# A second slot table: twelve of the 36 expert pairs moved in among the last chunks of a fused RWKV and mixture-of-experts kernel

## What is computed

```python
def attn(x):                       # an RWKV block on layernorm(x)
    xn = ln(x); xp = shift(xn)
    k, v, r = (mixes of xn and xp) @ Wk, Wv, Wr     # r through a sigmoid
    wkv = scan over the tokens of exp(k)*v and exp(k), one over the other
    x = x + r * wkv @ Wo
    yn = ln(x); kk = relu((0.5*yn + 0.5*shift(yn)) @ Wfk)**2
    return x + sigmoid(yn @ Wfr) * (kk @ Wfv)

def ffn(x):                        # experts, E = 8, H = 256, top 2
    top, idx = top_k(x @ gate_w.T, 2); p = softmax(top)
    h1, h2 = x @ w12[e]            # 2 x 256 columns
    out_e = (silu(h1) * h2) @ w3[e]
    return sum over the two chosen e of p_e * out_e

x = x + attn(layernorm(x)); return x + ffn(layernorm(x))
```

## Time and profile before

| what | value |
|---|---|
| median of 3 runs | 348.77 us (347.84 to 348.89) |
| the profiled execution's own time | 348.16 us |
| its span (first to last instruction) | 346.4 us |
| PE / PE weight load busy | 78% / 61% |
| DVE / ACT / POOL busy | 71% / 56% / 64% |
| granted TensorE clock, mean | 0.899 of full speed |

### The profile page before, as it was taken

One profiled execution on the slowest core, in us unless ns is written; L12 is line 12 of the kernel. 1 busy time (PEld: TensorE's weight loads), 2 busy tenths in 40 slices (PEclk: granted clock), 3 DMA queues, 4 the chain that ended last, 5 costly groups with the idle time before them and its releaser, 6 DMA issues.

```text
span 346.4 us, 6531 instructions
## 1 busy us (share of the span) xinstructions
PE 270.9 (78%) x1697; PEld 211.3 (61%) x1698; DVE 246.0 (71%) x742; ACT 195.6 (56%) x397; POOL 221.2 (64%) x251
## 2 busy tenths in 40 slices
PE   0388699999779699695949635599999999999700
PEld 0134366766547366373735422499999999999700
DVE  3089998989699796997724757066666666666794
ACT  2546578888828667185544322276666666767200
POOL 5233557557857688677788677426666666666680
PEclk9999899999969899697876965899999999999965
DMA  7920000000011110011001113323333333233785
GB/s 263 437 68 0 1 2 31 0 32 32 34 38 38 47 33 31 31 40 54 32 31 62 62 42 108 98 67 91 93 91 88 91 91 86 84 99 89 260 275 211
DMA packets 22411, 29.12 MB, mean 84 GB/s; under 512 B 4318, under 2 KB 15584, under 8 KB 22129
## 3 DMA queue, kind: packets, MB, share of 16 engines
q1 hardware_dynamic: 14832, 13.45, 13.0%
q0 software_dynamic: 4352, 8.47, 7.4%
q10 hardware_dynamic: 3200, 6.90, 5.3%
HBM read 15.09 MB, written 12.14 MB: 79 GB/s over the span
## 4 chain that ended last, share of the span: by engine, by line
issue 33%; POOL 32%; PE 12%; DMA 10%; DVE 7%; SPq 2%; ACT 1%; POOLq 1%; DVEq 0%; ACTq 0%
POOL res_d L429 11%; POOL rows_d L404 10%; DMA x_all<-x 5%; PE p_f L707 2%; POOL x L374 2%; PE p_up L695 2%; POOL rs L350 2%; DMA o_all<-res_d 2%; POOL ysum L381 2%; POOL x_all L358 2%; POOL gated L366 1%; PE p_up L778 1%; POOL rs L390 1%; PE p_up L656 1%; DMA res_d<-yo,result_row 1%
## 5 line engine op out<-in xcount | busy, mean ns | idle before, releaser
L429 POOL DMA_INDIRECT res_d<-yo,result_row x72 | 70.9, 985 | 40.9 <-issue 30.2
L404 POOL DMA_INDIRECT rows_d<-rows,pos x64 | 67.5, 1055 | 21.8 <-issue 21.2
L778 PE MATMUL p_up<-xgT,w_up 128*128 128x128 f32 x576 | 71.7, 279 | 0.0
L778 PEld LDWEIGHTS p_up<-xgT,w_up 128*128 128x128 f32 x576 | 68.6, 196 | 0.0
L1028 DVE SCALAR_TENSOR_TENSOR gate_h<-th,p_up 128x512 f32<-128x512 f32 x36 | 24.8, 688 | 41.3 <-ACT th L586 41.3
L601 ACT ACTIVATE w_up<-w_exp 128x512 f32 x72 | 41.3, 622 | 12.3 <-issue 11.4
L695 PE MATMUL p_up<-ysum,w_sb 128*128 128x512 f32 x64 | 38.5, 713 | 5.6 <-POOL ysum L381 5.6
L586 ACT ACTIVATE th<-p_up 128x512 f32<-128x512 f32 x36 | 21.5, 597 | 29.0 <-PE p_up L778 29.0
L707 PEld LDWEIGHTS p_f<-wfv_half,kk 128*128 128x128 f32 x256 | 30.9, 192 | 4.9 <-issue 4.3
L542 ACT ACTIVATE hr<-p_up 128x512 f32<-128x512 f32 x32 | 18.8, 587 | 26.2 <-PE p_up L695 26.2
L707 PE MATMUL p_f<-wfv_half,kk 128*128 128x128 f32 x256 | 32.1, 277 | 0.0
(11 more groups left out here) (150 smaller groups left out, 554.0 us busy)
## 6 DMA issues: line engine op xcount, KB each, us to landing
xg<-rows_d SPq DMA_DIRECT2D x72, 65.0 KB, 1.8
o_all<-res_d SPq DMA_DIRECT2D x16, 256.0 KB, 5.3
w_exp<-experts ACTq DMA_DIRECT2D x1, 3072.0 KB, 17.1
x_all<-x SPq DMA_DIRECT2D x10, 256.0 KB, 2.3
out<-x_all ACTq DMA_DIRECT2D x8, 256.0 KB, 2.5
x_all<-x SPq DMA_DIRECT2D x1, 1536.0 KB, 16.8
res_d<-yo,result_row POOLq DMA_INDIRECT x72
rows_d<-rows,pos POOLq DMA_INDIRECT x64, 2.4
```

The costliest lines, as they stand in the source:

```text
L404: pool.indirect_dma_start(out=rows_d[:, :], out_offset=bass.IndirectOffsetOnAxis(ap=row, axis=0), in_=rows_of[c % 2][:, t, k, :], in_offse ...
L429: pool.indirect_dma_start(out=res_d[:, :], out_offset=bass.IndirectOffsetOnAxis(ap=row, axis=0), in_=yo[u][:, n, :], in_offset=None, bound ...
L778: mm = pe.matmul(p_up[u % 2][:, n, h * P:(h + 1) * P], w_up[u % 2][:, n, h * P:(h + 1) * P], xgT[u % 2][:, n, :], start=True, stop=True)
```

## The change

The expert stage is split. `FIRST_SLOTS` = 24 slots (12 pairs) take full tiles of rows that the first four chunks have written. A first table is made for them from the counts after chunk 3, and the other 48 slots (24 pairs) get a second table after the last chunk. Pairs 0 to 8 are written by hand into the lists of all engines among turns 8 to 11. While chunks still need PSUM, pairs 0 to 4 (`SHARED_PAIRS`) use one half of `p_up`, `p_up[1]`, for their transposes, their up product and their down product alike, and the transposes of pair q wait for `yo_ready` of pair q-1. All loops over rounds are written out. Chunk results no longer go through a tile `x3` and a copy by DMA, but straight into `x_all`. The start of the first three pairs by `late_rows` is gone, and so are the warm-up products of PE ahead of `turn_m(7)` and of the expert stage. SP writes all eight pads. The core of the diff:

```diff
-EARLY = 3
+FIRST_CHUNKS = 4
+FIRST_SLOTS = FIRST_CHUNKS * CT * TOPK // P - E
+FIRST_PAIRS = FIRST_SLOTS // 2
+SHARED_PAIRS = 5
...
+        def up_bank(q):
+            return p_up[1 if q < SHARED_PAIRS else q % 2]
+        def turn_bank(q):
+            return p_up[1][:, 0, 0:2 * P] if q < SHARED_PAIRS else p_tr[:, 0:2 * P]
+        def down_bank(q, n):
+            return p_up[1][:, n, 0:D] if q < SHARED_PAIRS else (p_tok, p_f)[q % 2][:, n * D:(n + 1) * D]
...
+            sp.wait_ge(S["table_row"], 1)
+            sp.wait_ge(S["dispatched0"], 16 * TPC * TOPK * FIRST_CHUNKS // 2)
+            sp.wait_ge(S["dispatched1"], 16 * TPC * TOPK * FIRST_CHUNKS // 2)
+            for q in range(FIRST_PAIRS):
+                load(q)
             sp.wait_ge(S["total_int"], 1)
             sp.wait_ge(S["pads"], 3)
-            fill_pads(sp, range(0, E, 2))
...
+            fill_pads(sp, range(E))
+            sp.wait_ge(S["table_row"], 2)
             sp.wait_ge(S["dispatched0"], 16 * TPC * TOPK * CHUNKS // 2)
...
+            sp.wait_ge(S["dispatched1"], 16 * TPC * TOPK * CHUNKS // 2)
+            sp.wait_ge(S["pad_filled"], 16 * E)
+            sp.wait_ge(S["idle_filled"], 16)
+            for q in range(FIRST_PAIRS, PAIRS):
+                load(q)
...
-                pool.tensor_tensor(x3[:, :, :], ffn[:, :].rearrange("p (t d) -> p t d", t=TPC),
+                pool.tensor_tensor(x_all[:, tiles(c), :], ffn[:, :].rearrange("p (t d) -> p t d", t=TPC),
...
+                if q == 0:
+                    after(pe, "exp_done", CHUNKS)
+                elif q <= SHARED_PAIRS:
+                    after(pe, "yo_ready", q)
+                else:
+                    after(pe, "xgT_ready", q)
...
+            turned_rows(2)
+            relu(0)(7)
+            square(0)(7)
+            expert_weights(3)
+            relu(1)(7)
+            square(1)(7)
+            tanh(2)
...
+            first_table()
+            place(4)
+            ln3(5)
+            label(4)
+            ln3_apply(5)
+            ln2(7)
+            gate_hidden(0)
+            pick(5)
+            weigh(0)
+            gate_hidden(1)
+            gated_ffn(6)
+            place(5)
+            weigh(1)
...
+            pick(6)
+            gate_hidden(3)
+            weigh(3)
+            gate_hidden(4)
+            gated_ffn(7)
+            weigh(4)
+
+            place(6)
+            gate_hidden(5)
+            ln3(7)
+            label(6)
+            weigh(5)
+            ln3_apply(7)
```

More of the change, by code:

```diff
@@ L186, in build, with turns @@
         block = ctx.enter_context(nc.Block())
-        def pipeline(steps):
-            lags = [lag for _, lag in steps]
-            for i in range(min(lags), CHUNKS + max(lags)):
+        def turns(steps, first, last):
+            for i in range(first, last):
                 for step, lag in steps:
@@ L603, in next_expert_weights @@
-            def next_expert_weights(q, r, u):
-                if not isinstance(q, int) or q >= 2:
-                    expert_weights(q, r, u)
-            for q in range(2):
-                expert_weights(q, 0, q)
-            rounds(act, [(turned_rows, -1), (tanh, 0), (next_expert_weights, -2)], 1)
+            relu(0)(6)
+            square(0)(6)
+            expert_weights(0)
+            turned_rows(0)
+            relu(1)(6)
+            square(1)(6)
+            relu(2)(6)
+            square(2)(6)
@@ new lines, in _ @@
+            relu(2)(7)
+            square(2)(7)
+            normed_m(6)
+            turned_rows(3)
+            expert_weights(4)
+            tanh(3)
+            relu(3)(7)
+            square(3)(7)
+            gap_exp(6)
+            turned_rows(4)
+            copy_rows(6)
+            expert_weights(5)
+            tanh(4)
+            turned_rows(5)
+            expert_weights(6)
+            turned_rows(6)
+            tanh(5)
+            expert_weights(7)
+            normed_m(7)
+            turned_rows(7)
@@ new lines, in _ @@
+            gate_in(5)
+            r_in(7)
+            ffn_in(0)(5)
+            attn_out(6)
+            ffn_in(1)(5)
+            ffn_in(2)(5)
+            turn_m(4)
+            ffn_out(0)(5)
+            scores(4)
+            ffn_in(3)(5)
+            first_total()
+            ffn_out(1)(5)
+            ffn_out(2)(5)
+            ffn_out(3)(5)
+            turn_y(6)
+            ranks(4)
+            gate_in(6)
+            ffn_in(0)(6)
+            attn_out(7)
+            pe.wait_ge(S["experts_in"], 16)
@@ new lines, in _ @@
+            turn_rows(0)
+            ffn_in(1)(6)
+            ffn_in(2)(6)
+            up(0)
+            turn_m(5)
+            ffn_out(0)(6)
+            scores(5)
+            ffn_in(3)(6)
+            down(0)
+            ffn_out(1)(6)
+            turn_rows(1)
+            ffn_out(2)(6)
+            up(1)
+            ffn_out(3)(6)
+            turn_y(7)
+            ranks(5)
+            down(1)
+            gate_in(7)
+            turn_rows(2)
+            ffn_in(0)(7)
+            up(2)
@@ new lines, in _ @@
+            ffn_in(1)(7)
+            ffn_in(2)(7)
+            down(2)
+            turn_m(6)
+            turn_rows(3)
+            ffn_out(0)(7)
+            up(3)
+            scores(6)
+            ffn_in(3)(7)
+            ffn_out(1)(7)
+            down(3)
+            turn_rows(4)
+            ffn_out(2)(7)
+            up(4)
+            ffn_out(3)(7)
+            ranks(6)
+            down(4)
+            turn_rows(5)
+            up(5)
+            turn_rows(6)
+            up(6)
+            down(5)
@@ new lines, in _ @@
+            turn_m(7)
+            turn_rows(7)
+            up(7)
+            down(6)
+            scores(7)
+            turn_rows(8)
+            up(8)
+            down(7)
+            ranks(7)
+            turn_rows(9)
+            up(9)
+            down(8)
+            all_total()
+            turn_rows(10)
+            for q in range(10, PAIRS):
+                if q == FIRST_PAIRS - 1:
+                    up(q)
+                    down(q - 1)
+                    down(q)
+                    turn_rows(q + 1)
+                elif q == FIRST_PAIRS:
+                    turn_rows(q + 1)
+                    up(q)
+                else:
+                    if q + 1 < PAIRS:
+                        turn_rows(q + 1)
+                    up(q)
+                    down(q - 1)
```

361 lines of the change are left out of this document (211 added, 150 removed).

## The result

The changed kernel takes 360.9 us (median of 4 runs, 359.55 to 366.19), the kernel before 348.3 us on the same chip. The ratio is 1.035, 95% interval 1.030 to 1.041: slower by 3.5%. The forecast was slower, 352.0 us, range 343 to 360, so the sign was right and the size was not. The profiled execution took 359.92 us, its span is 358.2, the mean granted clock 0.909.

What follows compares the result with a forecast made beforehand. PE was taken to bound the expert stage, POOL's waits the stretch ahead of the last dispatch. From 348.16 us, 30.6 saved against 30.4 lost gives 348.0; 4 for the clock gives 352.0, range 343 to 360.

Steps and rivals of the forecast that it cites:

- The saving: Behind the last dispatch: only pairs 12 to 35 remain, so the last down product comes 30.6 us sooner after it.
- D: The end of POOL's last dispatch, 220.98 us in the kernel before; the prediction counts its saving and cost from it.
- SP's eight pads at 0.95 us each end before D does: Pad writes on SP: they can start when the totals are there, 10 us earlier, so they delay nothing.
- D = 251.4: End of the last dispatch at full clock, claimed 30.4 us later than 220.98.
- Up to `gated_ffn(7)`: Turns with shared-bank pairs 0 to 4, 43.9 us in sum: `gated_ffn(7)` ends at 212.1, 17.9 us later.
- From there to D: From `gated_ffn(7)` to the last dispatch: 39.3 us instead of 26.8, for scatters 7.6, `ln3(7)` 3.0, `label(7)` 1.9.
- The clock: PE's granted clock from 169 to 241 us: 0.78 would add 7.9 us, full clock nothing; middle taken, 4 us.
- rival 2: PE keeps the low clock in the chunk pipeline's last stretch: 355.9 us and a few more; chance 0.17.
- The table: First table on DVE: `slot_row` ready 3.0 us in, `place(4)` and `ln3(5)` start 3.5 us later.
- Rival 1: Pairs 0 to 4 hide in the chunks' waits, their extra 11.9 us vanish: 340.1 us; chance 0.27.
- That is the floor: 333.8 us, if the last dispatch moved only by POOL's ten scatters (12.7) and the table (3.5).
- The edits costed at nothing: Written-out loops, longer list, `x3` copies gone: 0; removed warm-ups could cost up to 5.8 us at pair 12, within the range.

Runs made afterwards that it cites:

- c5: Changed kernel with turn 11 cleared: most scatters behind the last dispatch, pads ahead of waiting loads, all five shared-bank pairs kept; 353.5 us, ratio 1.018.
- filled: Changed kernel plus 13 idle products (128x512, result unread) where PE waits anyway; 354.5 us, ratio 1.017.
- experiment 3: Changed kernel with DVE's `place(5)` moved behind `weigh(1)`; 360.5 us, ratio 1.034.
- c0: Changed kernel with no pair in turns 9 and 10 and turn 11 cleared as in c5; 341.2 us, ratio 0.979.
- late_table: c0 with the first table made behind `ln3_apply(6)` and ACT's wait for it moved ahead of the first expert copy; 338.0 us, ratio 0.969.
- k0: Changed kernel with pairs 0 to 4 out of turns 9 and 10, pair 0 starting where pair 5 stood, no shared bank; 355.5 us, ratio 1.018.
- c2: c0 with pairs 0 and 1 in the shared bank in turn 9; 347.4 us, ratio 0.998.
- late_smooth: late_table with pairs 11 and 12 in the common order, pipeline not emptied between them; 336.0 us, ratio 0.964.
- late_filled: late_smooth plus six idle PE products ahead of `turn_m(5)`, `turn_m(6)` and `ranks(7)`; 337.7 us, ratio 0.966.

## Why the prediction was right in its sign and wrong in its size

**The saving: right, 1.4 too large.** "The last down product ends at D + 77.0", and 30.6 saved. Measured: D + 78.9, and 29.2 saved. The pitch of 2.90 and PE without a gap were as said. The 1.9 us lie ahead of pair 12: its load was issued 3.2 us behind D instead of 1.6. Two things are in these 1.6 us. SP issues the load 0.9 us behind the wait that ends last, a step that the sum left out. And "SP's eight pads at 0.95 us each end before D does" did not hold: the totals were there 7.9 us before D and not 10, and the pads follow each other every 1.12 us, so the last is issued at D and has landed 2.3 us behind it. In c5, whose pads end before D, SP's wait for the rows ends 2.1 us behind D (the sum had 1.6) and the load is issued 2.9 behind D. So the pads are worth 0.3 us of the 1.6, and the rest is the landing and the step behind it.

**The step that failed: "D = 251.4", 255.4 with the clock.** The last dispatch ended at 262.0, 6.6 us later. The way the cost arises was as said (the shared-bank pairs put off `gated_ffn(7)`, and turn 11 the rest); the intervals of pairs 1 and 4, the moments' wait of POOL in turn 11, and the clock were sized too small. By its parts:

- *Up to `gated_ffn(7)`, "212.1 instead of 194.2".* It was 218.4. The run `filled`, whose clock is 0.98 and 0.96, gives 215.1, so 3.0 us were missing at full clock, and 3.3 belong to the clock. The intervals of pairs 0 to 4 were 11.3, 10.2, 9.4, 10.1 and 9.4 us; those predicted were 10.0, 7.6, 9.4, 10.0 and 6.9. Pairs 2 and 3 were right. Pair 0 had its two `ffn_in` at half clock (3.42 us), pair 1 the `place(5)` of experiment 3, which costs it 2.4, pair 4 an `ffn_out` at half clock and an up product partly at it (1.92 and 2.54 us). In `filled` pair 1 still takes 10.2 and pair 4 takes 7.8.
- *From there to D, "39.3".* It was 43.6, and 41.0 in `filled`. The three scatters were as said. `ln3(7)` behind `gate_hidden(5)` was to cost POOL 3.0 us more: from `gated_ffn(7)` to POOL's step behind the moments it was 10.4 us instead of 3.7, so 6.7 more. The wait for `label(7)` was 3.76 (predicted 1.9). c5 shows that all of the 16.8 us over before is what stands in turn 11, scatters and other engines' steps, since without them the stretch is 27.0.
- *The clock, "I take the middle, 4 us".* `filled` brings D 5.9 us earlier, and its clock is not yet full: from 240 us to D it is 0.78. The direction was right; rival 2 had 7.9, with the whole stretch at 0.78.
- *The table, "3.5 us later".* DVE's part was right, 3.55. In c0 its place costs 5.1 (against late_table). ACT's wait for `slot_w`, 4.39 us ahead of the `relu` that PE needs next, had no price in the sum; how much of the 5.1 is that wait, the collision of `place(5)` or the clock is open.

D was short by 6.6 us and the saving was 1.4 too large: 8.0 together, against 359.9 - 352.0 = 7.9. By `filled`, 4.7 of the 6.6 belong to the sum at full clock and 1.9 to the clock term; as the clock of `filled` was not full in the last 16 us ahead of D, the clock's part can be larger.

**Where the 41.0 us of D come from**, by differences of the runs, us: the first table 5.1 (c0 and late_table); the other changes ahead of `gated_ffn(7)` without a pair in turns 9 and 10, 2.5 (k0's 7.6, less the table; c0, with the same lists, gives 0.9); pairs 0 and 1, 0.1 (c0 and c2 give 3.2); pairs 2 to 4, 16.5 (c5 and c2 give 17.6); turn 11, 16.8. They sum to 41.0, as differences along one line of runs must. The two large terms are far beyond the spread of 1.6; the two small ones are not.

**Rival 1, pairs hidden in waits**, fell: the five pairs of the shared bank came every 10.1 us on the mean, not 6.4, and the text had named that interval as what would decide. "That is the floor; I see no list order that gives it" was not refuted, but late_smooth's 336.0 comes within 2.2 us of the 333.8, by another way: D stays at 220.9, with no scatter ahead of it, and 12.3 us are saved behind it.

**The edits costed at nothing.** The loops written out and the warm-ups removed at pair 12: the pitch stayed 2.90, and pair 12 ran its up product in 1.95 us. The pads on SP: some 0.3 us in after, as said above, and far more in k0, where they stood behind a load that waits for a buffer.

## What to carry to other kernels

Work that is moved into the gaps of a pipeline pays only if the chain that ends the pipeline stays where it is: compare what one piece costs ahead of its last step (here 5.5 us a pair in a shared bank, and 2.54 of POOL for its scatters) with what it saves behind it (2.90). Put nothing into the lists of the chain's last turns, and look on every engine for the instruction that waits for the new work's first input, not only on the one that makes it (here ACT ahead of `relu(0)(6)`; moving the table and that wait gave 5.1 us). An engine that was busy two thirds of the time in a chain of handovers was not free here for a second chain of handovers.

## What the runs showed of the hardware

- Two DVE products of 128x32 elements took 0.29 us together, 2.26 beside two of POOL's 128x512 sums (after) and 4.12 beside three (c0). Moving the step out of the way of pair 1 gave that pair 2.4 us and the kernel at most about 1 (experiment 3).
- Idle products in PE's waits raised the granted clock from 0.88 and 0.83 to 0.98 and 0.96, and D fell by 5.9 us. In late_filled the low level only moved to a later window, and the time did not fall.
- Between D and the end POOL can be the next limit: in c0 it scattered 22 tiles at a pitch of 1.28 us without a stop from D on. From pair 12 on PE was the limit again, with 2.90 us a pair.
- The pads, issued by SP, followed each other every 1.12 us in after, and the last had landed 2.0 us after SP began to wait for it.
